# Routing tokens to experts: a slot table summed in PSUM in place of lists scattered to memory

## The reference

```python
logits = t @ Wg.T + bg
idx = jnp.argmax(logits, axis=-1)
out = jnp.zeros_like(t)
for e in range(W1.shape[0]):
    mask = (idx == e).astype(t.dtype)[:, None]
    h = jax.nn.gelu(t @ W1[e].T + b1[e], approximate=False)
    y = h @ W2[e].T + b2[e]
    out = out + mask * y
```

## Time and profile before

| | us |
|---|---|
| three runs | 3069.05, 3075.79, 3080.05 |
| median | 3075.79 |
| the profiled execution, its own time | 3074.15 |
| its span in the profile | 3072.5 |
| mean granted TensorE clock, of 2.4 GHz | 0.927 |

### The profile page before, as it was taken

The page is one execution under the profiler, slowest core; times in us unless marked ns, Lnnn a source line. Parts: engine busy times, 40 slices in busy tenths (PEclk is TensorE's granted clock), DMA queues, the critical chain, the costliest instruction groups (busy, mean ns, idle before and its releaser), DMA issues. The chain is left out here.

```text
span 3072.5 us, 57265 instructions
## 1 busy us (share of the span) xinstructions
PE 2701.5 (88%) x20914; PEld 1026.6 (33%) x20914; DVE 2335.8 (76%) x3728; ACT 1938.2 (63%) x3195; POOL 904.5 (29%) x1426
## 2 busy tenths in 40 slices
PE   5887899999999999997799699999999999981776
PEld 4665122222222222221565222222222222271655
DVE  4554899999989999993364699999999999671222
ACT  2443176767767766766344399999999999920332
POOL 0011333333333333321423111111111111046776
PEclk9777599999999999999799799999999999975999
DMA  5675545445445445533455331111111111160221
GB/s 117 200 225 176 98 97 108 96 95 109 97 91 110 95 93 107 102 79 62 123 169 153 86 89 44 44 42 44 42 42 42 42 42 44 48 151 4 62 63 44
DMA packets 174506, 274.82 MB, mean 89 GB/s; under 512 B 59596, under 2 KB 109462, under 8 KB 169650
## 3 DMA queue, kind: packets, MB, share of 16 engines
q0 software_dynamic: 63360, 155.78, 22.6%
q1 hardware_dynamic: 110900, 115.76, 13.5%
HBM read 174.45 MB, written 97.39 MB: 88 GB/s over the span
## 5 line engine op out<-in xcount | busy, mean ns | idle before, releaser
L461 ACT ACTIVATE a_probs<-a_psS 128x1024 f32<-128x1024 f32 x768 | 744.2, 1021 | 378.2 <-PE a_psS L373 378.2
L938 DVE TENSOR_REDUCE a_halfmax<-a_psR 128x2 f32<-128x1024 f32 x768 | 884.3, 1217 | 12.9 <-PE a_psR L764 12.7
L886 ACT ACTIVATE a_probs<-a_psS 128x512 f32<-128x512 f32 x1536 | 835.0, 596 | 84.1 <-PE a_psS L780 66.6
L507 DVE TENSOR_REDUCE a_halfmax<-a_psR 128x1 f32<-128x512 f32 x768 | 492.6, 685 | 40.3 <-PE a_psR L355 37.4
L507 DVE TENSOR_REDUCE h_halfmax<-a_psR 128x1 f32<-128x512 f32 x768 | 490.5, 685 | 26.5 <-PE a_psR L355 23.6
L801 PE MATMUL a_psO<-a_probs,a_v 128*17 128x256 f32 x6144 | 482.1, 386 | 21.6 <-ACT a_outT L868 20.3
L373 PE MATMUL a_psS<-a_qrows,a_krows 121*128 121x512 f16 x1536 | 401.6, 383 | 40.2 <-DMA a_qrows<-relh 39.1
L384 PE MATMUL a_psO<-a_probs,a_v 128*17 128x512 f32 x3072 | 405.9, 600 | 0.6 <-ACT a_probs L461 0.6
L801 PEld LDWEIGHTS a_psO<-a_probs,a_v 128*17 128x17 f32 x6144 | 103.3, 95 | 321.3 <-ACT a_probs L886 263.9
L1290 PE MATMUL p_psQ<-p_xnT,p_wqk 96*128 96x512 f32 x384 | 188.3, 655 | 16.0 <-DVE p_xnT L1444 13.9
L373 PEld LDWEIGHTS a_psS<-a_qrows,a_krows 121*128 121x128 f16 x1536 | 119.9, 98 | 228.7 <-DMA a_qrows<-relh 60.8
(11 more groups left out here) (213 smaller groups left out, 3177.2 us busy)
## 6 DMA issues: line engine op xcount, KB each, us to landing
qk<-p_half SPq DMA_DIRECT2D x96, 256.0 KB, 3.4
a_qrows<-rel POOLq DMA_DIRECT2D x96, 256.0 KB, 4.4
a_qrows<-qk POOLq DMA_DIRECT2D x144, 128.0 KB, 4.8
a_v<-v POOLq DMA_DIRECT2D x96, 136.0 KB, 2.4
relh<-p_rel SPq DMA_DIRECT2D x48, 256.0 KB
attn<-a_out SPq DMA_DIRECT2D x96, 128.0 KB, 2.4
v<-p_v SPq DMA_DIRECT2D x36, 272.0 KB, 3.4
rel<-p_rel SPq DMA_DIRECT2D x36, 256.0 KB
```

The lines of the kernel that those rows point to most:

```text
L461: nc.scalar.activation(PT[:, blk % 2, 2 * pair:2 * pair + 2, :], psS[:, b0:b0 + 2, :], ACT.Exp, scale=scale).then_inc(exped, 1)
L507: nc.vector.tensor_reduce(mx[:, unit, half:half + 1], psR[:, slot, :], AX.X, ALU.max)\
L886: nc.scalar.activation(PT[:, blk % 2, o, :], psS[:, bank(m), :], ACT.Exp, scale=scale)\
L938: nc.vector.tensor_reduce(MX[:, unit:unit + UNITS // QH // 2 + 1:UNITS // QH // 2, kh], psR[:, slot, :].rearrange("p (r k) -> p r k", r=2) ...
```

## The change

The scatter to memory and the gather are gone. What remains is held in SBUF and PSUM:

- `choose(r)` now ends in the rank alone, its tile within the expert (`HI128`, rank shifted right by 7) and minus the rank inside that tile (`NLO`); `OH` is kept for all rounds.
- ScalarE, `place_tokens(r)`: for each of 16 columns a 128x128 matrix `LT` with the token's number plus 1 at its offset and 0 elsewhere, in two steps: square of (offset - rank in tile), then relu of (id1 - 2 id1 x that). 16 of one and then 16 of the other, a round.
- VectorE, after the tile ends: the first tile of each token's expert (`FT`, `TW`, `TN`), and then for each round the matrix `AT` with 1 at the token's tile, 128 x 16 x 80, written over the attention tiles that are no longer needed (named f_attn and r_attn).
- TensorE: 64 products `LT` x `AT` of 128x128 by 128x80, all summed in one PSUM bank. The sum at (slot, tile) is the number plus 1 of the token there.
- VectorE: zeros become `EMPTY`, and 1 is taken off; this writes `IXA`.

The diff, cut to its core (views of the whole tile are written as the tile's name, `nc.vector.` is left out):

```diff
@@ route, SP and GpSimd
-            sp.wait_ge(made, NMADE)
-            sp.dma_start(SLOTS.rearrange("(p n) o -> p (n o)", p=P), FILL[:, :]).then_inc(filled, 16)
...
-            nc.gpsimd.iota(EB[:, :, :], [[0, NT], [CAP, E_N]], ...)
-            nc.gpsimd.iota(IDF[:, :], [[P, ROUNDS * NT]], ...)
+            nc.gpsimd.iota(ID1[:, :], [[P, ROUNDS * NT]], base=1, channel_multiplier=1, **exact)
+            nc.gpsimd.iota(NID1[:, :], [[-2 * P, ROUNDS * NT]], base=-2, channel_multiplier=-2, **exact)
+            nc.gpsimd.iota(UP128[:, :], [[1, P]], base=0, channel_multiplier=0, **exact)
+            nc.gpsimd.iota(UPNT[:, :], [[1, NTILE]], base=0, channel_multiplier=0, **exact)
-            nc.gpsimd.memset(FILL[:, :], EMPTY).then_inc(made, 1)
...
-            for r in range(ROUNDS):
-                pool.wait_ge(ch, r * CH + CH)
-                list_tokens(r, 0, NT // 2)
-                if r + 3 < ROUNDS:
-                    root(r + 3)
-                list_tokens(r, NT // 2, NT)
-            pool.wait_ge(scat, ROUNDS * 16 * NT)
-            pool.wait_ge(fin, 15)
-            pool.indirect_dma_start(SL[:, :], None, SLOTS..., ROW...)
+            for r in range(ROUNDS):
+                root(r)
@@ route, TensorE
-            pe.wait_ge(fin, 16)
+            for r in range(ROUNDS):
+                pe.wait_ge(placed, r + 1)
+                pe.wait_ge(tiled, r + 1)
+                for t in range(NT):
+                    k = r * NT + t
+                    mm = nc.tensor.matmul(psT[:, 0, 0:NTILE], LT[:, k, :], AT[r // 2][:, NT * (r % 2) + t, :],
+                                          start=(k == 0), stop=(k == ROUNDS * NT - 1))
+            mm.then_inc(gathered, 1)
+            pe.wait_ge(fin, 13)
             nc.tensor.transpose(psC[0:1, 0:P], TL[:, :], ident[:, :]).then_inc(fin, 1)
-            pe.wait_ge(fin, 19)
-            nc.tensor.transpose(psK[:, 0:NTILE], SLF[:, :], ident[0:NTILE, 0:NTILE]).then_inc(fin, 1)
@@ route, ScalarE
+            def place_tokens(r):
+                act.wait_ge(ch, r * CH + CH)
+                for t in range(NT):
+                    a = nc.scalar.activation(LT[:, r * NT + t, :], UP128[:, :], ACT.Square, bias=NLO[:, r, t:t + 1], scale=1.0)
+                a.then_inc(squared, 1)
+                act.wait_ge(squared, r + 1)
+                for t in range(NT):
+                    k = r * NT + t
+                    a = nc.scalar.activation(LT[:, k, :], LT[:, k, :], ACT.Relu, bias=ID1[:, k:k + 1], scale=NID1[:, k:k + 1])
+                a.then_inc(placed, 1)
...
+                if r >= 2:
+                    place_tokens(r - 2)
+            for r in range(ROUNDS - 2, ROUNDS):
+                place_tokens(r)
@@ route, VectorE, end of choose(r)
-                link(tensor_tensor(PW, psK, EB, ALU.add))
-                link(tensor_tensor(PW, PW, OH, ALU.mult))
-                link(tensor_reduce(PO, PW, AX.X, ALU.add))
-                link(tensor_copy(POI[:, r, :], PO[:, :, 0]))
+                link(tensor_tensor(PW, psK, OH[:, r, :, :], ALU.mult))
+                link(tensor_reduce(RK, PW, AX.X, ALU.add))
+                link(tensor_copy(RKI, RK))
+                link(tensor_scalar(RKI, RKI, 7, None, ALU.arith_shift_right))
+                link(tensor_copy(HI128[:, NT * r:NT * r + NT, 0], RKI))
+                link(scalar_tensor_tensor(NLO[:, r, :], HI128, float(P), RK, ALU.mult, ALU.subtract))
@@ route, VectorE, after the tile ends
+            nc.vector.memset(FT[:, 0:1], 0.0)
+            step(8, tensor_copy(FT[:, 1:E_N], END[:, 0:E_N - 1]))
+            step(9, tensor_tensor(TW, OH, FT..., ALU.mult))
+            step(10, tensor_reduce(TN, TW, AX.X, ALU.add))
+            step(11, tensor_tensor(TN, TN, HI128, ALU.add))
+            for r in range(ROUNDS):
+                tensor_tensor(AT[r // 2][...], TN[...], UPNT[...], ALU.is_equal).then_inc(tiled, 1)
+            step(12, tensor_scalar(GE, END, JP, None, ALU.is_le))
+            step(13, tensor_reduce(TL, GE, AX.X, ALU.add))
+            dve.wait_ge(fin, 14)
+            step(15, tensor_scalar(TR, psC[0:1, 0:P], float(E_N - 1), None, ALU.min))
+            dve.wait_ge(gathered, 1)
+            step(16, tensor_scalar(GONE, psT[:, 0, 0:NTILE], 0.0, float(EMPTY), ALU.is_equal, ALU.mult))
+            step(17, scalar_tensor_tensor(IXA, psT[:, 0, 0:NTILE], -1.0, GONE, ALU.add, ALU.add))
```

More of the change, by code:

```diff
@@ L1537, in _, with route @@
             round_of(ROUNDS - 1, True)
-CAP = T
 NTILE = T // P + E_N
-LIST = E_N * CAP + NTILE * P
 CM = C + 2
 EMPTY = 1 << 20
-def route(nc, name, early, ON, WG, BG, X3, SLOTS, TR, IXA):
+def route(nc, name, early, ON, WG, BG, X3, TR, IXA):
     NT = PAIR // P
@@ L1578, in route @@
         EQ = sb("isTop", [P, NT, E_N])
-        OH = sb("chosen", [P, NT, E_N])
+        OH = sb("chosen", [P, ROUNDS, NT, E_N])
         PRE = [sb(f"chosenUpTo{i}", [P, NT, E_N]) for i in range(2)]
@@ L1582, in route @@
         DESC = sb("descending", [P, NT, E_N])
[L1583 to L1588, removed]
+        PW = sb("ranks", [P, NT, E_N])
+        RK = sb("rank", [P, NT, 1])
+        RKI = sb("rankInt", [P, NT], I32)
+        HI128 = sb("rankTile", [P, ROUNDS * NT, 1])
+        NLO = sb("minusRankInTile", [P, ROUNDS, NT])
+        ID1 = sb("tokenIdsFrom1", [P, ROUNDS * NT])
+        NID1 = sb("minusTwiceTokenIds", [P, ROUNDS * NT])
+        UP128 = sb("upTo128", [P, P])
+        UPNT = sb("upToTiles", [P, NTILE])
+        LT = sb("tokenAtOffset", [P, ROUNDS * NT, P])
+        FT = sb("firstTile", [P, E_N])
+        TW = sb("firstTileOf", [P, ROUNDS * NT, E_N])
+        TN = sb("tileOf", [P, ROUNDS * NT, 1])
+        AT = [o[:, :, :, :, :].rearrange("p b g t c -> p (b g t c)")[:, 0:2 * NT * NTILE]
+              .rearrange("p (t n) -> p t n", n=NTILE) for o in Os]
+        GONE = sb("unfilled", [P, NTILE])
         TRI = sb("before", [P, P])
@@ L1613, in route @@
         wload = sem("wload")
-        filled = sem("filled")
+        squared = sem("squared")
+        placed = sem("placed")
+        tiled = sem("tiled")
+        gathered = sem("gathered")
         oload = [early.ol, sem("oload")]
@@ L1624, in route @@
         rk = sem("rk")
-        scat = sem("scat")
-        ids = sem("ids")
         fin = sem("fin")
-        slots = sem("slots")
         rsq = sem("rsq")
         NPRE = NT.bit_length() - 1
-        CH = 16 + NPRE
+        CH = 18 + NPRE
         NM = 4
-        NMADE = 12
+        NMADE = 13
         def tiles(r):
@@ L1686, in root @@
                     .then_inc(rsq, 1)
[L1688 to L1697, removed]
-            for r in range(ROUNDS):
-                pool.wait_ge(ch, r * CH + CH)
-                list_tokens(r, 0, NT // 2)
-                if r + 3 < ROUNDS:
-                    root(r + 3)
-                list_tokens(r, NT // 2, NT)
-            pool.wait_ge(scat, ROUNDS * 16 * NT)
-            pool.wait_ge(fin, 15)
-            pool.indirect_dma_start(SL[:, :], None, SLOTS.rearrange("(r p) o -> r (p o)", p=P),
-                                    bass.IndirectOffsetOnAxis(ap=ROW[0:NTILE, 0:1], axis=0)).then_inc(slots, 16)
+            for r in range(ROUNDS):
+                root(r)
         @block.tensor
@@ L1739, in ranks @@
                 pe.wait_ge(ch, r * CH + 9)
-                nc.tensor.matmul(psK[:, 0:NT * E_N], TRI[:, :], OH[:, :, :].rearrange("p t e -> p (t e)"),
+                nc.tensor.matmul(psK[:, 0:NT * E_N], TRI[:, :], OH[:, r, :, :].rearrange("p t e -> p (t e)"),
                                  start=True, stop=False)
@@ L1833, in choose @@
                     link(nc.vector.tensor_tensor(new[:, d:NT, :], old[:, d:NT, :], old[:, 0:NT - d, :], ALU.add))
-                link(nc.vector.tensor_tensor(RUN[:, :], PRE[NPRE % 2][:, NT - 1, :], OH[:, NT - 1, :], ALU.add))
+                link(nc.vector.tensor_tensor(RUN[:, :], PRE[NPRE % 2][:, NT - 1, :], OH[:, r, NT - 1, :], ALU.add))
                 dve.wait_ge(rk, r + 1)
                 link(nc.vector.tensor_tensor(PW[:, :, :], psK[:, 0:NT * E_N].rearrange("p (t e) -> p t e", e=E_N),
[L1837 to L1840, removed]
+                                             OH[:, r, :, :], ALU.mult))
+                link(nc.vector.tensor_reduce(RK[:, :, :], PW[:, :, :], AX.X, ALU.add))
+                link(nc.vector.tensor_copy(RKI[:, :], RK[:, :, 0]))
+                link(nc.vector.tensor_scalar(RKI[:, :], RKI[:, :], 7, None, ALU.arith_shift_right))
+                link(nc.vector.tensor_copy(HI128[:, NT * r:NT * r + NT, 0], RKI[:, :]))
+                link(nc.vector.scalar_tensor_tensor(NLO[:, r, :], HI128[:, NT * r:NT * r + NT, 0], float(P), RK[:, :, 0],
+                                                    ALU.mult, ALU.subtract))
                 assert n[0] == CH
@@ L1865, in _ @@
             step(7, nc.vector.tensor_copy(END[:, :], psK[:, 0:E_N]))
[L1867 to L1879, removed]
@@ L1880, in _ @@
-            step(19, nc.vector.tensor_copy(SLF[:, :], SL[:, :]))
-            dve.wait_ge(fin, 20)
```

(24 more changed lines are left out.)

19 lines of the change are left out of this document (7 added, 12 removed).

## The result

| | before | changed |
|---|---|---|
| median of 4 and 4 runs, us | 3077.92 | 3054.73 |
| lowest and highest | 3069.05, 3080.40 | 3049.42, 3059.54 |
| ratio, with 95% interval | | 0.9937 [0.9920, 0.9955] |
| the profiled execution | 3074.15 | 3056.76 |
| its span | 3072.5 | 3055.1 |

Faster by 0.6%, 19 us by the ratio. The forecast was 3046, with 3037 to 3062 as range; the rival "the clock stays at the half" had given 3058.

A forecast was written before the change was run, and what follows sets the result against it. The scatter queue and gather were taken to bound the end of `route`; with the terms, the table is complete at 2808.9 instead of 2837.97, -29.1 us, so 3046 as median, range 3037 to 3062, the forecast's own 3038 to 3053.

The forecast's parts named there:

- the clock stays at the half: Rival for the 64 products: all 128 passes at 0.21 us, 27 us instead of 15.7; 17.8 us gained, 3058; chance 0.17.
- the rival with 0.43 us a pass: Rival for the 64 products: each pass costs what a 256-column pass costs, 55 us in all; slower, 3086; chance 0.03.
- What bounds the kernel: End of `route`: VectorE waits 46.6 us for gathered slot rows; 52.4 us from last choice to table that no arithmetic fills.
- Start of route, -0.9: Start of `route`: GpSimd's changed iotas and memset and VectorE's dropped cast save 0.9 us, as VectorE waits there.
- The rounds, +0.3: Rounds of `route`: VectorE's changed operations add 0.17 us each; only rounds 2 and 3 count, +0.3 us.
- ScalarE's 0.35 us an activation: `place_tokens`: 32 activations a round at 0.35 us each, 11 us a round, hidden behind other work.
- From the last choice to the first product: End of `route`: tile ends, then VectorE's `FT`, `TW`, reduce, `TN` and first `AT`, from 2785.0 to 2791.7.
- A pass costs what its weights cost: The 64 products: 128 passes, each 0.21 us at half clock or 0.105 at full, set by weights, not the 80 columns.
- The clock rises after 4.5 us: The 64 products: 21 passes at 0.21 us, then 107 at 0.105 after TensorE's clock rises; 15.7 us in all.
- the rival with 0.17: Rival that TensorE's clock stays at the half during the 64 products: 27 us, 17.8 us gained, 3058; chance 0.17.
- The end: After the last product: transpose and copy, 0.8 us, and two 80-column operations, 0.24 us each; from 2807.5 to 2808.9.
- `experts` moves as a block: Stage after `route`: set by its 160 indirect DMAs before and after, so it shifts by what `route` gains or loses.

The follow-up runs named there:

- b_few: Kernel before the change, only the last column of each round scattered (4 of 64 scatters): 8.2 us from last choice to table instead of 52.4.
- the list kernel: The kernel before the change, which scatters the token list to memory and gathers it: median 3077.92 us, 52.4 us from last choice to table.
- e_half: Changed kernel with both matrices in float16, token numbers counted within the round, one bank per round: median 3040.29 us, 0.9883 of the kernel before.
- e_wide128: Changed kernel with 128 columns instead of 80 in all 64 products: burst 17.1 us, table 26.4 us after the last choice.
- e_warm: Changed kernel with eight unread 256-column products ahead of the burst: burst 14.3 us, 22.7 us from choice to table; timed, 0.9930 of the kernel before.
- e_double: Changed kernel with the loop of 64 products run twice: 62.8 us from choice to table, 54.7 us of products at clock 0.50.

## Why the prediction was right and where it was not

- **The number.** The median, 3054.73, lies in the stated range of 3037 to 3062, but only because that reached out to the low clock; the forecast's own range, 3038 to 3053, it misses. (Two small slips in the prediction: 3075.79 - 29.1 is 3047, not 3046, and in the rival with 0.43 us a pass `IXA` comes 10.2 later, not 9.8.)
- **What bounds the kernel.** Right. b_few shows it alone: with 4 scatters the 52.4 us are 8.2.
- **Start of route, -0.9.** Right: VectorE's first addition starts 2.53 us after the first row of `route` instead of 3.47. But see the rounds.
- **The rounds, +0.3.** Wrong by 3.1 us for the stretch from the start of `route` to the last choice: forecast 90.9 - 0.9 + 0.3 = 90.3, measured 93.4. With the -0.9 of the start right, the term that stood at +0.3 came out at +3.4. What I left out is that these rounds are TensorE's, whose clock changes inside them. The largest part is in the logits of round 1, here before and changed:

```profile
2725.04 10.15 PE L1734 MATMUL r_psL<-r_wg,r_xT 96*128 96x16 f32 x64 [1.06 <-ACT r_xT L1768]
...
2723.62 12.63 PE L1716 MATMUL r_psL<-r_wg,r_xT 96*128 96x16 f32 x64 [0.95 <-ACT r_xT L1769]
```

Before, the clock stood at 1.00 for the first 4 us of that row, in the changed kernel for less than 2 us. Over all runs one round's logits took 9.7 to 12.8 us. In the ten other runs with the change or an edit of it the stretch falls into three groups, 90.4 to 90.9 (two), 93.3 to 93.6 (four) and 96.1 to 96.2 us (four); in both runs of the list kernel, b_few being the other, it is 90.9. Whether the change shifts it or only meets it otherwise was not tried.
- **ScalarE's 0.35 us an activation.** 0.30 for the square (4.81 for 16), 0.39 for the relu (6.26): 11.1 us a round against 11.2. `place_tokens(0)` ends at 2755.5 and the copies of round 3 start at 2757.9, so it is hidden, with 2.3 us to spare. Round 3 is placed 12.3 us after the last choice, forecast 11, and hidden as forecast.
- **From the last choice to the first product.** 6.72 us, forecast 6.8.
- **A pass costs what its weights cost.** Right in number: 0.21 at the half clock with 16, 40, 80 and 128 columns, 0.11 at the full; a fixed cost of each pass it is not, since the float16 products of e_half took under 0.08 us each at the half clock. That the time is the loading of the weights is inferred: no run changes the weights alone. The sentence of the Trainium skill ("TensorE: Matmul & The Clock Gate", "The mechanism", the section ahead of the one that the prediction names), that a weight load overlaps products in flight only in another row group, doesn't agree with this trace: 40 columns more or less change nothing.
- **The clock rises after 4.5 us.** This step failed. It stayed at 0.50 for all 27.4 us: 11.7 us too much, and that is the forecast's miss at the table (35.4 against 23.9). I had read two kinds of rows, columns at which the clock fell (16) and columns at which it rose (128 and more), and leaned to the rise because `experts`, busy 79% of the time, keeps 1.00. But from 2870 to 3000 the clock was high already: that stretch shows only that it was held. It had risen between 2854 and 2856, where TensorE was busy throughout, on products of 128 columns and more. e_wide128, e_warm and e_double separate the two: these products hold a raised clock and don't raise a low one. So the rival with 0.17 was the one that came true. That its 17.8 us and the span's 17.4 agree so closely is partly luck, since the rounds and what the next point tells make up for each other.
- **The end.** 1.36 us, forecast 1.4. The start of `experts` is 0.5 us behind the table, where it was 3.0, which I had not seen coming; the prediction had taken the 3 us for what a barrier costs. With the 0.7 us by which `route` starts sooner it makes up for the rounds.
- **`experts` moves as a block.** In this pair, 231.6 and 231.8. But in the eight other runs whose table is complete the same work took 226.0 to 233.3 us, so a single pair shows it only within some 7 us.

## What to carry to other kernels

Indices that fit in SBUF need no trip through memory: a one-hot matrix product places them, here 64 products for 64 indirect DMAs of 1.3 us each. Ask then what a product costs by its weights and its number of passes as well as by its columns: here 40 to 128 columns cost the same, and float16 on numbers kept small enough to be exact took all but the last 0.75 us of the burst off the path. And read from a trace separately at what work TensorE's clock rises and at what it only stays; where the engine waits anyway just ahead of a burst, wide unread products there can pay (12 us at the table here), though making the burst short pays more.

## What the runs showed of the hardware that I had not expected

- The same float32 products of 80 columns ran at 1.2 GHz for 54.7 us, and at 2.4 GHz for 28.5 us once wide ones had raised it. The Trainium skill ("TensorE: Matmul & The Clock Gate", "Why this matters for your kernels") tells that a continuously busy TensorE gets the full clock; in the record TensorE is busy all of the 54.7 us, and it doesn't.
- More work was faster: 128 columns 17.1 us, 80 columns 27.4.
- Four operations of 1280 columns on VectorE, on broadcast operands, took 5.70 us with float32 and with float16.
- Between the table and the first row of `experts` were 3.0 us with 64 scatters, 0.5 with 4 of them and 0.5 in all eleven runs without. Why is open; nothing was tried on it alone.
